# Sixteen tiles' attention products moved to the seam between two transformer layers

## The reference

```python
xn = layernorm(x)
x = x + L0_attn(xn) + L0_ffn(xn)   # attention without softmax, 16 heads, rotary; 8 experts, top 2 per token
xn = layernorm(x)
x = x + L1_attn(xn) + L1_ffn(xn)   # softmax attention in blocks of 64, 8 heads; 8 experts, each takes its 512 best tokens
```

## Time and profile before

| | |
|---|---|
| median of 3 runs | 783.04 us (782.2 to 786.39) |
| the profiled execution | 782.92 us, of which the span is 781.2 us |
| PE busy | 735.1 us, 94% |
| DVE busy | 565.0 us, 72% |
| ACT busy | 399.1 us, 51% |
| POOL busy | 455.8 us, 58% |
| share of the chain that ended last | PE 81%, DVE 11%, issue 3%, ACT 2% |

### The profile page before, as it was taken

One profiled execution on the slowest core, in us unless ns is written; L12 is line 12 of the kernel. 1 busy time (PEld: TensorE's weight loads), 2 busy tenths in 40 slices (PEclk: granted clock), 3 DMA queues, 4 the chain that ended last, 5 costly groups with the idle time before them and its releaser, 6 DMA issues.

```text
span 781.2 us, 19641 instructions
## 1 busy us (share of the span) xinstructions
PE 735.1 (94%) x6336; PEld 655.4 (84%) x6336; DVE 565.0 (72%) x1265; ACT 399.1 (51%) x873; POOL 455.8 (58%) x577
## 2 busy tenths in 40 slices
PE   6999999999999999999995999799989889999994
PEld 4888854989999999999995999777678678888983
DVE  4888863887787777776757887489899756676642
ACT  4445444444544444444444888546668565544411
POOL 3777777998867767974432223023367635666363
PEclk9999999999999999999997999889999999999998
DMA  9799543344434443443339787234447765666342
GB/s 260 209 270 291 179 134 89 88 137 128 114 116 125 117 123 108 127 118 109 101 87 300 253 278 212 48 66 110 108 101 175 214 227 133 145 147 146 60 51 30
DMA packets 149057, 113.99 MB, mean 146 GB/s; under 512 B 59359, under 2 KB 139234, under 8 KB 148964
## 3 DMA queue, kind: packets, MB, share of 16 engines
q1 hardware_dynamic: 135764, 86.94, 39.9%
q0 software_dynamic: 12624, 25.35, 12.8%
q10 hardware_dynamic: 576, 0.53, 0.3%
HBM read 68.68 MB, written 40.80 MB: 140 GB/s over the span
## 4 chain that ended last, share of the span: by engine, by line
PE 81%; DVE 11%; issue 3%; ACT 2%; POOL 1%; DMA 0%; DVEq 0%; POOLq 0%; ACTq 0%
PE bank L860 15%; PE banks L878 12%; PE bank L1117 11%; PE bank L934 6%; PE banks L1128 5%; PE banks L734 4%; PE bank L741 3%; PE banks L799 3%; PE banks L949 3%; PE banks L788 3%; PE bank L1025 2%; PE bank L847 2%; PE bank L1008 2%; DVE rw L1666 1%; PE bank L997 1%
## 5 line engine op out<-in xcount | busy, mean ns | idle before, releaser
L860 PE MATMUL bank<-rw,rt 128*128 128x128 f32 x1136 | 139.0, 275 | 3.3 <-DVE rt L1658 2.6
L860 PEld LDWEIGHTS bank<-rw,rt 128*128 128x128 f32 x1136 | 132.5, 192 | 5.2 <-DVE rt L1658 3.9
L878 PE MATMUL banks<-r_split,rt_split 128*128 x852 | 118.8, 289 | 0.1
L2102 POOL DMA_INDIRECT ults_by_choice_and_token<-rw,y_id x71 | 79.6, 1121 | 66.2 <-ACT rw L1280 60.5
L878 PEld LDWEIGHTS banks<-r_split,rt_split 128*128 128x128 f32 x852 | 106.1, 190 | 0.3 <-issue 0.3
L1672 DVE TENSOR_TENSOR rt_split<-rw,rt_split 128x512 fp32r<-128x512 f32 x71 | 61.8, 870 | 48.7 <-ACT rt_split L1273 48.7
L1273 ACT ACTIVATE rt_split<-rw 128x512 fp32r<-128x512 f32 x71 | 44.8, 630 | 92.3 <-DVE rw L1666 91.5
L1666 DVE TENSOR_TENSOR rw<-rw 128x512 f32<-128x512 f32 x71 | 74.1, 1044 | 24.4 <-ACT rw L1267 23.9
L1117 PE MATMUL bank<-r_split 128*128 128x512 f32 x384 | 89.6, 391 | 1.3 <-issue 1.1
L1117 PEld LDWEIGHTS bank<-r_split 128*128 128x128 f32 x384 | 71.4, 188 | 16.3 <-issue 1.9
L2202 POOL DMA_INDIRECT out_x<-r,idx x32 | 50.2, 1569 | 52.9 <-DVE r L1960 45.2
(11 more groups left out here) (253 smaller groups left out, 1575.3 us busy)
## 6 DMA issues: line engine op xcount, KB each, us to landing
rt<-in_w SPq DMA_DIRECT2D x24, 512.0 KB, 4.7
rw<-rows_by_expert SPq DMA_DIRECT2D x71, 128.0 KB
r<-in_w SPq DMA_DIRECT2D x16, 512.0 KB, 6.0
r<-ults_by_choice_and_token SPq DMA_DIRECT2D x32, 256.0 KB, 3.8
rw<-in_x SPq DMA_DIRECT2D x16, 256.0 KB, 4.2
rw<-in_sin_q SPq DMA_DIRECT2D x32, 128.0 KB
rw<-x_layer SPq DMA_DIRECT2D x16, 256.0 KB
x_plus_bias<-rw SPq DMA_DIRECT2D x16, 256.0 KB, 2.9
```

The costliest lines, as they stand in the source:

```text
L860: last = pe.matmul(bank[1 + t % 2][:, k * P:(k + 1) * P], c_w1[:, t % 2, c, k * P:(k + 1) * P], c_xT[:, t % 2, c, :], start=c == 0, stop=c ...
L878: last = pe.matmul(bank[6 + t % 2][:, 0:D], h[:, t % XB, c, :], w[:, ds(e2, 1), o + c * D:o + (c + 1) * D], start=n == 0, stop=n == 3 * HC ...
L2102: pool.indirect_dma_start(y0_d[:, :], bass.IndirectOffsetOnAxis(y_id[:, t:t + 1].bitcast(I32), 0), c_y[:, t % XB, :], None, bounds_check=l ...
```

## The change

Sixteen late tiles in place of eight (`NE` = `NT` - 16): tiles 16 to 23, whose products stood in the loop at steps 47 to 66, now have them in the seam as well. The first sixteen keep their steps. The late tiles are loaded at steps 46 to 68, one or two steps apart, and get their bias at the same steps. They lie in the place of the queries of tiles 0 to 15, where the experts' results lay before; `d_y` moves to the memory of the loop's weight copies and high parts and has three buffers instead of four. SyncE loads three units of results ahead instead of four; the fourth is loaded behind the store of unit 0.

In the seam, TensorE does the bias product behind tile 24, and VectorE puts its sum and all of unit 0's combination between the additions of tiles 25 to 31. TensorE then does the projections of unit 0 ahead of the transposition of unit 1. ScalarE's program is as before.

The second value buffer is cleared ahead of the barrier, and VectorE's constants of the search are made ahead of it; `bit_f` moves to other memory for that.

```diff
-        NE = NT - 8
+        NE = NT - 16
...
-        o_step = [4 + (i * 65) // NE for i in range(NE)]
-        l_step = [max(0, k - 5) for k in o_step] + [62, 62, 64, 64, 67, 68, 70, 71]
+        o_step = [4 + (i * 65) // 24 for i in range(NE)]
+        l_step = [max(0, k - 5) for k in o_step] + [46 + 3 * i // 2 for i in range(NT - NE)]
...
-            return xT_all[:, :, (i - 8) * P:(i - 7) * P]
+            return xT_all[:, :, (i - NE) * P:(i - NE + 1) * P]
...
-        d_y = [r3f[:, o:o + 4 * TOPK * D].rearrange("p (b k i n) -> p b k i n", b=2, k=TOPK, i=2) for o in (0, N)]
+        d_y = rt[:, 0:3 * L // 2].rearrange("p (b k i n) -> p b k i n", b=3, k=TOPK, i=2)
...
@@ sync @@
             def load_xq(i):
                 if i >= NE:
-                    sp.wait_ge(ao_ps, i - 7)
+                    sp.wait_ge(ao_ps, i - NE + 1)
...
             def load_y(u):
-                if u >= 4:
-                    sp.wait_ge(x1_r, 2 * (u - 4 + 1))
+                if u >= 3:
+                    sp.wait_ge(x1_r, 2 * (u - 3 + 1))
...
-            sp.wait_ge(ao_ps, NT // 2)
             for i in range(XB):
                 sp.wait_ge(y_out[i], 16 * len(range(i, ST0, XB)))
-            for u in range(4):
+            for u in range(3):
                 load_y(u)
             for i in range(NE, NT):
                 store_x1(i)
...
             for u in range(NU):
                 store_unit(u)
-                if u >= 1 and u - 1 + DB < NU:
-                    load_x1(u - 1 + DB)
-                    load_y(u - 1 + DB)
+                if u + 3 < NU:
+                    if u >= 1:
+                        load_x1(u + 3)
+                    load_y(u + 3)
...
@@ tensor @@
-            for i in range(NE, NT):
-                attend(i)
...
             def values_scores(v):
                 if v.at_least(1):
                     pe.wait_ge(bo1_ps, 2)
+                else:
+                    pe.wait_ge(ao_sb, NT)
...
-            bias_of_values()
-            pe.wait_ge(ao_sb, NT)
+            for i in range(NE, NT):
+                attend(i)
+                if i == NT - 8:
+                    bias_of_values()
             transpose_unit(Unit(0, 0, 2))
-            for u in (1, 2, 3):
+            project_before(Unit(0, 1, 2))
+            transpose_unit(Unit(0, 1, 2))
+            for u in (2, 3):
                 transpose_unit(Unit(u // 2, u % 2, 2))
                 project_before(Unit(u // 2, u % 2, 2))
...
@@ vector @@
-            for i in range(NE, NT):
-                add_attention(i)
...
-            dve.wait_ge(bo1_ps, 1)
-            dve.tensor_tensor(bo1_s[:, :], bo1_s[:, :], bank[7][:, 0:D], ALU.add).then_inc(bo1_ps, 1)
+            for i in range(NE, NT):
+                add_attention(i)
+                if i == NT - 7:
+                    dve.wait_ge(bo1_ps, 1)
+                    dve.tensor_tensor(bo1_s[:, :], bo1_s[:, :], bank[7][:, 0:D], ALU.add).then_inc(bo1_ps, 1)
+                elif i in (NT - 6, NT - 4):
+                    combine(0, (i - NT + 6) // 2)
+                elif i == NT - 3:
+                    moments_unit(0)
+                elif i == NT - 2:
+                    scale_unit(0)
             for u in range(NU + 1):
-                if u < NU:
+                if 1 <= u < NU:
                     combine(u, 0)
                     combine(u, 1)
                     moments_unit(u)
                     scale_unit(u)
                 if u >= 1:
                     low_xT(u - 1)
+            dve.tensor_copy(bit_f[:, 1:NT], bit_i[:, 1:NT])
+            dve.memset(bit_f[:, 0:1], -1.0)
+            link(dve.memset(thr[:, :], 0))
+            dve.sem_inc(thr_r, 1)
             end_stage(dve, 3)
...
@@ gpsimd @@
-                if u == NU - 3:
-                    clear_v(0)
+                if u >= NU - 3 and u < NU - 1:
+                    clear_v(u - NU + 3)
             end_stage(pool, 3)
-            clear_v(1)
```

More of the change, by code:

```diff
@@ L224, in two_layers @@
         s_dig = scratch([2, SC], BF16)
-        bit_f = scratch([NT])
         onesf = scratch([P])
@@ L371, in two_layers @@
                       for o in (3 * L // 2 + 4 * D, 3 * L // 2 + 8 * D))
-        dy_in = [sem(f"expert_results_loaded_{i}") for i in range(4)]
+        dy_in = [sem(f"expert_results_loaded_{i}") for i in range(3)]
         x1_r = sem("x1_complete")
@@ L393, in two_layers @@
         e_av = work([2, NH1 * VC]).rearrange("p b (h d) -> p b h d", d=VC)
+        bit_f = work([NT])
         e_part = sb("e_part", [P, 2], BF16)
@@ L590, in load_y @@
             def load_y(u):
-                if u >= 4:
-                    sp.wait_ge(x1_r, 2 * (u - 4 + 1))
+                if u >= 3:
+                    sp.wait_ge(x1_r, 2 * (u - 3 + 1))
                 for k in range(TOPK):
                     o = k * N + 2 * u * P
-                    sp.dma_start(d_y[u // 2 % 2][:, u % 2, k, :, :], y0_d[o:o + 2 * P, :].rearrange("(i p) n -> p i n", p=P))\
-                      .then_inc(dy_in[u % 4], 16)
+                    sp.dma_start(d_y[:, u % 3, k, :, :], y0_d[o:o + 2 * P, :].rearrange("(i p) n -> p i n", p=P))\
+                      .then_inc(dy_in[u % 3], 16)
             def store_unit(u):
@@ L1705, in combine @@
                 dve.wait_ge(xg_in[u % 4], 32 * len(range(u % 4, ST0, XB)) + 16 * (u // 4 + 1))
-                dve.wait_ge(dy_in[u % 4], 32 * (u // 4 + 1))
-                x_t, y_t = d_x[:, u % DB, i, :], d_y[u // 2 % 2][:, u % 2, :, i, :]
+                dve.wait_ge(dy_in[u % 3], 32 * (u // 3 + 1))
+                x_t, y_t = d_x[:, u % DB, i, :], d_y[:, u % 3, :, i, :]
                 mark(dve.scalar_tensor_tensor(x_t, y_t[:, 0, :], top_w[:, 0, t:t + 1], x_t, ALU.mult, ALU.add))
@@ L1809, in step_e @@
                                       over_last(e_rc[:, b.par, :], DK), ALU.mult).then_inc(o_sb, 1)
-            dve.tensor_copy(bit_f[:, 1:NT], bit_i[:, 1:NT])
-            dve.memset(bit_f[:, 0:1], -1.0)
-            link(dve.memset(thr[:, :], 0))
-            dve.sem_inc(thr_r, 1)
             dve.wait_ge(rank1, 1)
```

## The result

The changed kernel is slower: median 785.49 us (783.99 to 788.75, 20 runs) against 782.34 us (781.06 to 786.39, 20 runs), ratio 1.0042 with a 95% interval of 1.003 to 1.0054, about +3.2 us or 0.4%. Forecast were 780.9 us, in a range of 777.8 to 784.8.

The account below looks back on a forecast made before the run. TensorE was taken to bound the expert loop and the second layer's projections, not the seam between. Loop's end and seam together -1.5 us, behind the barrier -0.56: -2.1 from 783.04 gives 780.9 us, range 777.8 to 784.8.

Parts of the forecast that it names:

- The loop's end: End of the first layer's expert loop: 6.91 us off for eight products and 0.44 more, 7.35 us earlier, at 396.49.
- a product taken out of this loop gives its whole price back: Expert loop, TensorE full: each attention product removed saves its 0.87 us, eight save 6.91 us.
- the lump: Four late tiles' loads and bias additions coming together in the old loop; spreading them out saves TensorE's 0.44 us idle.
- unit 0's projections at 6.38 us: Second layer's first projections, after the seam: length left at the old 6.38 us, partly at 1.2 GHz.
- the low clock through unit 1: Rival: TensorE's clock stays low or falls again before unit 1's queries and keys, 2.1 us; 783.0 to 784.4; chance 0.22.
- from the loop's end to the last addition: First part of the seam, sixteen late products with unit 0's combination between additions: 16.06 us, 8.69 more than before.
- on to unit 0's queries and keys: Seam, from VectorE's last addition to unit 0's first projections: 4.5 us, before 10.67, so 6.17 us less.
- from unit 1's transposition to its queries and keys: TensorE's pause behind unit 0's projections, waiting mainly for ScalarE's work in program order: 3.3 us added.
- behind the barrier: Before the search: a cast and two small fills go, the copy of the scores starts 0.56 us earlier.
- SyncE's queue: Sixteen stores in a row, then unit 3's load at about 416.5; rival: stores slow, unit 3 late, 788.3 us, chance 0.06.

Follow-up runs that it names:

- deep seam, late and timed: Changed kernel with units 0 and 1 interleaved further among late products, late bias additions moved to steps 59 on, behind VectorE's square; 774.67 us, 0.9906 of the kernel before.

## Why the prediction was wrong

- *The loop's end* is the step that failed: "a product taken out of this loop gives its whole price back", and the lump is "the only place where I see the loop's bound give way". Forecast -7.35, measured -3.6: 3.76 us, of which 0.33 is the later start and 3.47 the steps 47 to 69 (82.77 us, 79.30 by the forecast). I read from TensorE's 159.56 busy us of 160 that nothing else was near the bound. But the products themselves were the cover: in a step without one VectorE's chain has 0.6 us to spare, and an addition of GpSimd beside the square takes 1.0. The rows of the lump showed the mechanism, and I priced only the lump, and that too low: the step behind it (65, 4.14 us) is 0.7 longer than bare steps, not 0.44. What the Trainium skill's page "SBUF — State Buffer", section "SBUF: two separate sides", says of the lock holds for every single addition and not only for four in a row; I did not carry it on to the twelve others. With the additions moved, the loop gives 7.22 us (86.65 to 79.43), so a product does give its whole price back once nothing stands beside the square.
- *The clock* was the other one: I left unit 0's projections at 6.38 us (5.98 measured) and gave the low clock through unit 1 a chance of 0.22. It fell twice, and unit 1's queries and keys took 4.61 us for 2.83: 1.8 us. Mechanism and price (2.1 us) of that rival were near enough. Its chance was too low: it came in four of seven traces of this seam, and where it didn't, the first low stretch was longer. By itself the second fall would have left the forecast at 782.7 us; the loop alone would have brought it to 784.7.
- *Right within 0.2 us:* from the loop's end to the last addition 16.26 us (forecast 16.06), on to unit 0's queries and keys 4.41 (4.5), from unit 1's transposition to its queries and keys 3.19 (3.28), behind the barrier 0.55 (0.56). SyncE's queue was at 417.97 (416.5) behind sixteen stores of 0.72 us each; VectorE waited for no load.
- The sum: -2.1 forecast, +3.76 for the loop, +1.8 for the second low clock, -0.4 for the shorter first one, and less than 0.1 for the rest: +3.1, and +3.15 between the medians.

## What to carry to other kernels

An engine that is full to 99.7% may still be the cover of a chain just behind it: before taking work off it, subtract that work from the step and see whether the other engines' chain, with its worst neighbour, still fits. Work moved into a gap pays only if the waits that made the gap lie beside it, so plan the waiting engine's order first, and keep TensorE's pauses short, since each one may be paid again in its clock: here the two cost 3.0 us of a seam of 36.7.

## What the runs showed of the hardware

- A GpSimd addition of 0.75 us (128x256, both inputs in SBUF) beside a square on VectorE (128x512) makes the square last to 0.56 us behind the addition, 1.68 us in place of 0.69; a weight copy of 0.69 us lasted 2.47, to 0.56 us behind the third of four rotation products. Put behind the square, the same addition costs VectorE's next instruction 0.05 us (0.74 for 0.69). This is what the Trainium skill's page "SBUF — State Buffer", section "SBUF: two separate sides", says of the exclusive lock as far as the waiting goes. By that section whichever instruction starts first keeps the ports to its end; here the square is recorded as starting 0.37 us before the addition, and in the earlier trace rows 0.11 us before, and ends behind it. The measurement decides; whether the recorded start is the start of the lock no run shows.
- Steps 47 to 69 of one program agree to 0.03 us each between two executions on different chips whose totals differ by 15 us (783.99 and 799.06). Earlier, step 9 took 5.64 us in one and 4.30 in the other.
- The granted clock fell to 1.2 GHz in TensorE's pauses of 5.5 us (before) and 3.4 us (changed kernel), and 0.4 us into the queries and keys behind its pause of 2.4 us. Behind the same pause it stayed at 2.4 GHz in three other traces, and it did so throughout the seam with waits of up to 1.1 us (deep seam, late and timed).
